# Convolution stage of a fused expert network on one Trainium2 core: return DMAs on two queues, a norm chain one unit earlier, five low parts on GpSimd

## What is computed

```
x = x + MLP0(_gn(x))     # per channel e: gelu(x[:, e] @ w1[e] + b1[e]) @ w2[e] + b2[e], hidden size 1024
x = x + Conv(_gn(x))     # 3x3, 8 to 8 channels, edge padding, weights sign(w) * mean(|w|), plus bias
x = x + MLP2(_gn(x))     # like MLP0
x = x + MLP3(_gn(x))     # like MLP0, with the exact gelu
```

## Time and profile before

| | |
|---|---|
| median of 3 runs | 618.31 us (617.82 to 618.72) |
| the profiled execution | 618.62 us, span 616.8 us |
| granted TensorE clock, mean over the span | 0.994 |
| PE busy | 593.6 us, 96% of the span |
| DVE busy | 427.5 us, 69% |
| ACT busy | 417.2 us, 68% |
| POOL busy | 36.1 us, 6% |
| chain that ended last | PE 86%, DVE 5%, SP's queue 3%, DMA 3%, ACT 1%, POOL 1% |

### The profile page before, as it was taken

One profiled execution on the slowest core, in us unless ns is written; L12 is line 12 of the kernel. 1 busy time (PEld: TensorE's weight loads), 2 busy tenths in 40 slices (PEclk: granted clock), 3 DMA queues, 4 the chain that ended last, 5 costly groups with the idle time before them and its releaser, 6 DMA issues.

```text
span 616.8 us, 8582 instructions
## 1 busy us (share of the span) xinstructions
PE 593.6 (96%) x2893; PEld 496.5 (80%) x2893; DVE 427.5 (69%) x898; ACT 417.2 (68%) x706; POOL 36.1 (6%) x57
## 2 busy tenths in 40 slices
PE   8999999999999877799999999999999999999997
PEld 7788888888899656788888888888888888888885
DVE  5687898867677876596866865865866766675532
ACT  4777676767667431577767767778777777777743
POOL 2000000000000660000000000000000000000000
PEclk9999999999999998999999999999999999999999
DMA  8772565355453244423241322324224234234001
GB/s 256 215 225 104 136 170 161 108 173 146 141 163 93 68 113 115 153 76 131 68 138 69 111 94 83 123 69 136 70 75 164 87 98 158 87 100 156 17 19 68
DMA packets 56894, 73.05 MB, mean 118 GB/s; under 512 B 4201, under 2 KB 50443, under 8 KB 56850
## 3 DMA queue, kind: packets, MB, share of 16 engines
q1 hardware_dynamic: 56850, 72.50, 38.0%
HBM read 59.71 MB, written 8.59 MB: 111 GB/s over the span
## 4 chain that ended last, share of the span: by engine, by line
PE 86%; DVE 5%; SPq 3%; DMA 3%; ACT 1%; issue 1%; POOL 1%; DVEq 0%; ACTq 0%
PE G L1011 41%; PE ACC L1028 13%; PE ACC L1033 13%; PE ACC L1029 13%; SPq L460 2%; DMA NAT<-in_x 2%; PE ACC L1047 1%; DVE XC L834 1%; DMA W1raw<-in_L_conv_w 1%; PE TR L1060 1%; DVE Cl L826 1%; DVE BN L684 1%; PE TR L971 1%; POOL CN L542 0%; PE TR L1047 0%
## 5 line engine op out<-in xcount | busy, mean ns | idle before, releaser
L758 DVE TENSOR_TENSOR Hl<-HR,Hh 128x512 fp32r<-128x512 f32 (+1 forms) x208 | 134.1, 645 | 159.8 <-ACT Hh L609 158.8
L605 ACT ACTIVATE HR<-G,BT 128x512 f32<-128x512 f32 (+1 forms) x208 | 136.4, 656 | 143.3 <-PE G L1011 143.2
L1011 PE MATMUL G<-Xh,W1l 128*128 128x512 f32 (+1 forms) x416 | 160.2, 385 | 2.4 <-issue 2.4
L1011 PE MATMUL G<-Xh,W1h 128*128 128x512 f32 (+1 forms) x416 | 155.1, 373 | 0.0
L1028 PE MATMUL ACC<-Hh,W2l 128*128 128x512 f32 (+1 forms) x416 | 153.9, 373 | 0.0
L1029 PE MATMUL ACC<-Hh,W2h 128*128 128x512 f32 (+1 forms) x416 | 153.7, 373 | 0.0
L1011 PE MATMUL G<-Xl,W1h 128*128 128x512 f32 (+1 forms) x416 | 151.3, 374 | 0.1
L609 ACT ACTIVATE Hh<-HR 128x512 fp32r<-128x512 f32 (+1 forms) x208 | 124.7, 600 | 6.6
L1033 PE MATMUL ACC<-Hl,W2h 128*128 128x512 f32 (+1 forms) x416 | 121.9, 374 | 0.9 <-DVE Hl L758 0.8
L1011 PEld LDWEIGHTS G<-Xh,W1l 128*128 128x128 f32 x416 | 78.4, 188 | 14.9 <-issue 2.6
L1028 PEld LDWEIGHTS ACC<-Hh,W2l 128*128 128x128 f32 x416 | 78.3, 188 | 14.1
(11 more groups left out here) (87 smaller groups left out, 362.8 us busy)
## 6 DMA issues: line engine op xcount, KB each, us to landing
W2raw<-in_L_conv_w SPq DMA_DIRECT2D x24, 1024.0 KB, 5.5
W1raw<-in_L_conv_w SPq DMA_DIRECT2D x34, 512.0 KB, 4.5
W1raw<-in_L_conv_w SPq DMA_DIRECT2D x7, 1024.0 KB, 5.2
XC<-x_scratch SPq DMA_DIRECT2D x16, 304.0 KB, 6.1
x_scratch<-XT SPq DMA_DIRECT2D x16, 256.0 KB
out_x<-OUTT SPq DMA_DIRECT2D x16, 256.0 KB, 2.2
XT<-XC SPq DMA_DIRECT2D x30, 112.0 KB
NAT<-in_x SPq DMA_DIRECT2D x6, 512.0 KB, 7.5
```

The source lines that it names most:

```text
L605: nc.scalar.activation(HR[:, u % 2, 0:n], G1[u % 2][:, 0:n], act_of_layer, bias=BT1[:, f, col:col + 1]).then_inc(gelu_done, 1)
L758: nc.vector.tensor_tensor(Hl[:, u % RING, 0:n], HR[:, u % 2, 0:n], Hh[:, u % RING, 0:n].bitcast(F32), ALU.subtract).then_inc(hlo, 1)
L1011: ins = nc.tensor.matmul(G1[u % 2][:, 0:n], w[:, par, c, col], rhs, start=i == 0, stop=i == len(parts) - 1)
```

## The change

It splits `give_back`: SP issues the DMAs of the first block of each tile, ACT those of the second block, three tiles behind its high parts (BEHIND = 3), with those of the last three tiles after its loop. GpSimd writes the low part of tiles 2, 5, 8, 14 and 16 right behind the normalisation of the following tile, with a semaphore of its own. The chain of batch 1's first group in pass PC has its sums, mean, variance and scale one unit earlier and its eps two; the split of its input and of the first weight piece of expert 9 move with it. At the start nine of the eleven filler products are left out, the four transposes and their evictions stand two units later, the sums of that job at unit 6, and one weight piece (AHEAD = 4) is moved into the units. The core of the diff:

```
+BEHIND = 3
+LOW_ON_POOL = (2, 5, 8, 14, 16)
...
-            at[unit(PC, 7)] = (p, b)
+            at[unit(PC, 6)] = (p, b)
...
-AHEAD = 5
+AHEAD = 4
...
-            steps = [3, 4, 4, 5, 6, 6, 7, 7]
+            steps = [4, 4, 5, 5, 6, 6, 7, 7]
...
-            steps = [unit(PC, 5), unit(PC, 7)] + [unit(PD, t) for t in (1, 2, 3, 5, 6, 7)]
+            steps = [unit(PC, 6), unit(PC, 7)] + [unit(PD, t) for t in range(1, 7)]
...
-    (2, BOTH, -1, dict(sums=4, aggregate=5, mean=7, variance=8, eps=8, scale=9)),
+    (2, BOTH, -1, dict(sums=6, aggregate=6, mean=7, variance=8, eps=8, scale=9)),
...
-    (0, (1,), 0.5, dict(sums=unit(PC, 3), aggregate=unit(PC, 3), mean=unit(PC, 4), variance=unit(PC, 5),
-                        eps=unit(PC, 6), scale=unit(PC, 6))),
+    (0, (1,), 0.5, dict(sums=unit(PC, 2), aggregate=unit(PC, 2), mean=unit(PC, 3), variance=unit(PC, 4),
+                        eps=unit(PC, 4), scale=unit(PC, 5))),
...
+            def conv_low(q):
+                w = tile_width(q)
+                pool.wait_ge(chi, q + 1)
+                nc.gpsimd.tensor_tensor(Cl[:, q % CRING, 0:w], CN[:, q % CRING, 0:w],
+                                        Ch[:, q % HRING, 0:w].bitcast(F32), ALU.subtract).then_inc(clo_pool, 1)
...
                         for q in range(b * TILES, (b + 1) * TILES):
                             normalise_tile(q)
+                            if q - 1 in LOW_ON_POOL:
+                                conv_low(q - 1)
...
+            def give_back(q):
+                b, own = blocks(q)
+                if own.stop - own.start < 2:
+                    return
+                act.wait_ge(cadded, q + 1)
+                for j, n, c, g, i in rows_back(own.stop - 1):
+                    nc.scalar.dma_start(XT[GROUPS * i + g:GROUPS * (i + n):GROUPS, c, :, b],
+                                        XC[j * C:(j + n) * C, b, own.stop - 1, 1:N + 1]).then_inc(x2_in[b], 16)
...
                     for q in range(B * TILES):
                         conv_high(q)
+                        if q >= BEHIND:
+                            give_back(q - BEHIND)
                         if q == FIRST["split"]:
                             x_hi(PC, 0)
+                    for q in range(B * TILES - BEHIND, B * TILES):
+                        give_back(q)
...
                     if i == KS:
-                        pe.wait_ge(clo, q + 1)
+                        n, m = lows(q)
+                        if q in LOW_ON_POOL:
+                            pe.wait_ge(clo_pool, n)
+                        else:
+                            pe.wait_ge(clo, m)
...
-            for b in range(B):
-                stay_busy(4)
-                pe.wait_ge(xn_done, b + 1)
-            stay_busy(3)
+            pe.wait_ge(xn_done, B)
+            stay_busy(2)
...
-                if E == 0 and t < 4:
-                    x_transpose(4 + t)
+                if E == 0 and 2 <= t < 6:
+                    x_transpose(2 + t)
```

More of the change, by code:

```diff
@@ L219, in blocks, with lows @@
     return b, slice(2 * i, min(2 * i + 2, NBLK))
+def lows(q):
+    n = sum(1 for i in LOW_ON_POOL if i <= q)
+    return n, q + 1 - n
 def tile_width(q):
@@ L335, in build @@
         cn_done, chi, clo, conv_mm, cadded = (sem("cn_done"), sem("chi"), sem("clo"), sem("conv_mm"), sem("cadded"))
+        clo_pool = sem("clo_pool")
         mean_fixed = sem("mean_fixed")
@@ L457, in give_back @@
                 sp.wait_ge(cadded, q + 1)
[L458 to L461, removed]
+                for j, n, c, g, i in rows_back(own.start):
+                    sp.dma_start(XT[GROUPS * i + g:GROUPS * (i + n):GROUPS, c, :, b],
+                                 XC[j * C:(j + n) * C, b, own.start, 1:N + 1]).then_inc(x2_in[b], 16)
             for E in range(2, C + 1):
@@ L647, in _ @@
                         conv_high(q)
+                        if q >= BEHIND:
+                            give_back(q - BEHIND)
                         if q == FIRST["split"]:
                             x_hi(PC, 0)
+                    for q in range(B * TILES - BEHIND, B * TILES):
+                        give_back(q)
                 gelu(u)
-                if E == 0 and t in (0, 2):
-                    x_evac(4 + t)
+                if E == 0 and t in (2, 4):
+                    x_evac(2 + t)
                 for weight in WEIGHTS_AT.get(u, ()):
@@ L910, in _ @@
                 h_lo(u)
-                if E == 0 and t in (1, 3):
-                    x_evac(4 + t)
+                if E == 0 and t in (3, 5):
+                    x_evac(2 + t)
                 for weight in WEIGHTS_AT.get(u, ()):
@@ L919, in _ @@
                     if steps.get("sums") == u and "early" not in steps:
-                        if u == 4:
+                        if u == 6:
                             for i in (7, 8):
```

## The result

The changed kernel takes **615.40 us** (median; 613.23 to 619.37) beside 618.27 us (617.15 to 620.65) for the kernel before on the same chip: a ratio of 0.9954, 95% interval 0.9942 to 0.9967. It is faster, as forecast, but by 2.9 us where 8.5 were forecast, and 615.40 lies above the upper end of the forecast range (614.3). The profiled execution took 615.6 us, with a span of 613.8.

What follows compares the result with a forecast made beforehand. Time to issue the return DMAs was taken to bound the convolution stage. The start's 1.75 us plus 6.75 us up to pass PD make 8.5 us, from 618.62 to 610.1, as a median 609.8; range 605.3 to 614.3.

Steps and rivals of the forecast that it cites:

- What bounds the kernel: Convolution stage: the time to issue 44 return DMAs on SP, 0.83 us each, holds it, not the transfer.
- The start: Fewer fillers let g1(0) begin 2.0 us earlier; 1.75 us gained, bounds 0 and 3.45.
- PE waits 1.7 us and 1.75 us are left: At unit 7, PE is ready at 35.1 but DVE's later sums bring the mean's input at 36.8.
- The first half of the convolution: Tiles 0 to 9: POOL's low parts delay the power and CST, tile 10 starts at 222.2; loses about 1.5 us.
- The second half: From tile 10: DVE no longer waits for returns; g1(PC, 0) starts at 239.4 instead of 244.12.
- 1.3 + 0.6 us for sums, bias and aggregate: DVE's work from 228.8, after tiles 10 to 13, giving the mean at 230.8.
- PE waits 1.3, too short to lose the clock: At the mean of 230.8, PE waits 1.3 instead of 4.84 us and keeps its clock.
- PC and PD: Last passes: 1.0 us new gelu wait, earlier chain and w1 of expert 9; PD at 252.05 instead of 258.80.
- (a): Rival: PE stays the bound in the convolution, POOL collisions rarer, tile 10 at 219; 606.8 us, chance 0.27.
- (b): Rival: POOL's low parts take 2.2 us, low 2 and 5 hold PE up, CST later; 613.5 us, chance 0.17.
- (c): Rival: the two queues don't run side by side, 1.6 us an issue on ACT; 622.2 us, chance 0.08.
- (d): Rival: no change, PD still waits for the chain or w1 and the start gives nothing; 618 us, chance 0.06.

Runs made afterwards that it cites:

- e2: Kernel before with the new start alone: 619.15 us, ratio 1.0013 (0.9998 to 1.0028).
- e1: Changed kernel with the start of the kernel before put back: 613.22 us, ratio 0.9919.
- e3: Changed kernel with tile 16's low part given back from GpSimd to DVE: 613.72 us, ratio 0.9933.
- e7: Changed kernel with the old start and no low parts on GpSimd: 611.40 us, ratio 0.9877.
- e5: Kernel before with the return DMAs split over the SP and ACT queues alone: 612.08 us, ratio 0.9892.
- e6: Changed kernel with batch 1's chain, its split and the weight steps as before: 615.52 us, ratio 0.9950.
- e9: Changed kernel with the sums of the job of channels 2 and 3 ahead of unit 6's two low parts of weights: 613.55 us, ratio 0.9922.
- e11: e10 with the split of pass PC's input one tile later: 610.84 us, ratio 0.9876.
- e4: Changed kernel with eight filler products before the mean behind tile 14: 613.73 us, ratio 0.9925.
- e8: Changed kernel with old start, tile 16's low part on DVE, six fillers before the mean behind tile 14, three before tile 0: 611.28 us, ratio 0.9879.
- e10: e7 with five filler products before the mean behind tile 14 and three before tile 0: 611.07 us, ratio 0.9884.
- e12: e11 with the new start and e9's order of the sums: 608.46 us, ratio 0.9845.

## Why the prediction was wrong in size

**What bounds the kernel** was right: time to issue. The two queues took the DMA wait away and alone gained 6.3 us. What failed are two steps of the walk: the order of DVE's work at the start, and DVE's time for sums, bias and aggregate beside POOL's low part.

**The start** failed: 1.75 us were forecast and about 0.7 lost (e2, whose interval takes in no loss; by e1 the loss is 2.2). The step g1(0) two us earlier was right. The step "PE waits 1.7 us and 1.75 us are left" failed: PE was ready 0.8 us later than walked and DVE later by 1.2, and what was left was 0.3 to 0.4 us. Then the step that is missing altogether: after an idle time of 2 us at unit 7 the clock fell in two of five profiles, which cost 1.6 us more. The forecast asked that question for the mean FIRST and not here. The difference of e2 from the forecast is about 2.5 of the missing 5.6 us.

**The first half of the convolution** was too pessimistic. The issue on ACT is 0.83 (0.8 taken), the low part 1.31 (1.4 taken; the estimate by the ratio of 1.96 in the Trainium skill, GPSIMD Engine Reference, "Performance versus the Vector engine", was 1.35). But CST came 15.37 us after tile 0 (14.49 before, 16.9 forecast) and tile 10 after 17.26 (18.4 forecast, 16.84 before): 0.4 us lost, not 1.5. POOL's walk added up collisions that didn't happen: the five normalisations of tiles 4 to 8 took 4.2 us, not 5.9, and the power 0.56, not 0.93.

**The second half** failed in one step: "1.3 + 0.6 us for sums, bias and aggregate". With POOL's low part beside them they took 3.0 us, so that the mean came exactly when forecast (27.0 us after tile 0) although tile 10 was 1.1 us ahead, and "PE waits 1.3, too short to lose the clock" became 2.30 and a lost clock. From that mean to g1(PC, 0) the forecast had 8.6 us; e3, at full clock, takes 9.2 and after 10.7: 0.6 of walk and 1.55 of clock, 2.1 us in all. In e3 the stage takes 48.04 us where 48.2 was forecast.

**PC and PD** were right: ACT issues until 244.3, gelu(PC, 0) right behind it; the mean waits 1.30; no wait for w1 of expert 9, though it was issued at 245.1 and not at 241; PD 12.48 us behind g1(PC, 0), 12.65 forecast.

2.5 and 2.1 make 4.6 of the 5.6 us; with e1's figure for the start it is about 6. The difference is about the size of the medians' own uncertainty, and stays open. In the profiled execution the sum closes in another way: of the 5.5 us between its span and the forecast one (616.8 - 8.5 = 608.3), 2.05 are its late first mean, 1.31 are missing up to unit 7, 0.16 up to tile 0 and 2.00 in the stage. The other executions need not share that. The five of them with a granted clock of 0.989 or 0.990 took 616.85 to 619.37 us, the fifteen at 0.993 to 0.996 took 613.23 to 617.11: what is lost at the low clock differs from one execution to the next, and the profile (0.996) is one of those that lost little.

**The rivals.** (a), PE the bound at 606.8, didn't come: collisions on POOL were rarer, but it needed tile 10 at 219, 15.2 us after tile 0, and tile 10 came 17.26 us after it. (b) named the right suspect, POOL's low parts, at the wrong place: tiles 2, 5 and 8 together put tile 10 only 0.4 us later than before (0.8 later in e1 than in e7, which differ by them); tile 16's cost more. (c) is refuted by the issue of 0.83 us beside SP's: the Trainium skill (DMA: Bandwidth & Descriptors, "Issuing engines are not separate DMA queues") says that only the time to issue is saved, usually small. Here 44 issues of 0.83 us are 36 us, and dividing them over two queues gained 6.3 us (e5). (d), no change, is refuted.

## What to carry to other kernels

Cost a part of a change by what runs beside it as well as by its own length: five low parts were moved to relieve an engine, and one of them held that engine up on the path. Where steps are moved earlier, walk the engine that feeds the next rendezvous too; the two queues alone gained 6.3 us, while the earlier start gained nothing as long as DVE's sums came late, and with the sums moved too it was still no faster than the old start. An idle time near 2 us of PE is worth its length and perhaps 1.6 us more, so look for the longest one that is left.

## What the runs showed of the hardware that I had not expected

- Two DVE instructions on 128x2 elements took 1.36 us beside a two-input GpSimd operation, 0.82 beside one-input ones and 0.36 where GpSimd was nearly idle; in fourteen profiles the time goes with the low parts on GpSimd.
- TensorE's clock after an idle time: it fell to the lower level after 2.29 to 2.31 us (after, e1, e6, e9: each time), in 2 of 5 profiles after 1.97 to 2.17, and held after 1.43 to 1.75 but for one in e11. At tile 0, after a wait of 0.9 us behind short products with gaps, it fell in three of the nine changed kernels without fillers there (e1, e4, e7), and in none of the four with them (e8, e10, e11, e12).
- Between 222 and 232 us the packets of the two queues took 56 to 57% of the DMA engines' time for each MB in e10 and e11, and 34 to 41% in the ten other kernels with two queues, e9 and e12 on the same chip among them. Nothing in the edits goes with it.
